# A softplus sum and its product in four chunks each, between the scans, in a state-space and expert kernel

## The reference, cut to what matters

```
xc = silu(conv(xi) + conv_b)
dt, Bm, Cm = split(xc @ W_x)
dt = softplus(dt @ W_dt + b_dt)
dA  = exp(dt[..., None] * A)
dBu = (dt * xc)[..., None] * Bm[:, :, None, :]
h   = scan over tokens of  h = dA * h + dBu
y   = einsum('blds,bls->bld', h, Cm) + D_skip * xc
```

## Time and profile before

| what | value |
|---|---|
| median of 3 runs | 1552.35 us (1552.22, 1552.35, 1558.31) |
| profiled execution, its own time | 1550.88 us |
| span of its trace | 1549.1 us |
| DVE busy | 1218.7 us (79%), 2149 instructions |
| PE busy (matmuls) | 1324.8 us (86%) |
| POOL busy | 1046.6 us (68%) |
| ACT busy | 786.5 us (51%) |

### The profile page before, as it was taken

The page is one execution under the profiler, slowest core; times in us unless marked ns, Lnnn a source line. Parts: engine busy times, 40 slices in busy tenths (PEclk is TensorE's granted clock), DMA queues, the critical chain, the costliest instruction groups (busy, mean ns, idle before and its releaser), DMA issues.

```text
span 1549.1 us, 26016 instructions
## 1 busy us (share of the span) xinstructions
PE 1324.8 (86%) x8010; PEld 1071.6 (69%) x8010; DVE 1218.7 (79%) x2149; ACT 786.5 (51%) x1385; POOL 1046.6 (68%) x943
## 2 busy tenths in 40 slices
PE   8567776877877998898798799979799999999997
PEld 3245465565565766657566666868799989999997
DVE  3798999999989899999999998988355545555554
ACT  3676767867866786786787687666000000000000
POOL 3585878899989789889999988987433452122222
PEclk9696998989969899999999999989999999999999
DMA  7212111323214344344343333677867797676672
GB/s 221 78 53 83 48 49 56 97 75 88 86 65 136 113 120 128 82 142 143 106 127 110 85 114 109 189 230 230 287 179 202 215 251 213 195 206 195 192 206 79
DMA packets 129345, 216.36 MB, mean 140 GB/s; under 512 B 17948, under 2 KB 74792, under 8 KB 129080
## 3 DMA queue, kind: packets, MB, share of 16 engines
q1 hardware_dynamic: 110376, 183.86, 38.6%
q0 software_dynamic: 16064, 27.62, 7.7%
q10 hardware_dynamic: 2768, 3.21, 0.8%
HBM read 178.34 MB, written 37.22 MB: 139 GB/s over the span
## 4 chain that ended last, share of the span: by engine, by line
PE 48%; DVE 16%; POOL 13%; ACT 10%; issue 9%; DMA 3%; SPq 1%; DVEq 0%; POOLq 0%; ACTq 0%
PE psum L1712 14%; PE psum L1728 13%; POOL dBu L883 9%; DVE w_sb L2013 8%; PE psum L1514 7%; ACT psum L1137 3%; DVE y L2024 3%; PE psum L1523 2%; PE psum L1480 2%; ACT hc L1121 2%; PE psum L1680 2%; PE psum L1667 2%; POOL rows_d L801 1%; POOL gT L732 1%; DVE w_sb L1994 1%
## 5 line engine op out<-in xcount | busy, mean ns | idle before, releaser
L883 POOL TENSOR_TENSOR dBu<-w_sb,brep 128x512 f32<-128x512 f32 x512 | 644.5, 1323 | 34.8 <-issue 16.0
L2013 DVE TENSOR_TENSOR_SCAN w_sb<-psum,dBu 128x512 f32<-128x512 f32 x512 | 611.2, 1211 | 57.5 <-ACT psum L1137 38.1
L1137 ACT ACTIVATE psum<-w_sb,aneg 128x512 f32<-128x512 f32 x512 | 350.4, 692 | 116.9 <-DVE w_sb L2013 114.4
L1514 PE MATMUL psum<-ident,w_sb 128*128 128x128 f32 x2048 | 303.3, 295 | 117.0 <-DVE y L2024 70.0
L1514 PEld LDWEIGHTS psum<-ident,w_sb 128*128 128x128 f32 x2048 | 248.3, 151 | 192.7 <-DVE y L2024 102.9
L870 POOL DMA_INDIRECT out<-dBu,token x59 | 92.3, 1564 | 303.6 <-DVE dBu L2229 152.5
L1121 ACT ACTIVATE hc<-psum,ct 128x512 f32<-128x512 f32 x256 | 175.1, 684 | 102.8 <-PE psum L1514 69.4
L1523 PE MATMUL psum<-ident,hc 128*128 128x128 f32 x1024 | 171.7, 299 | 33.5 <-ACT hc L1121 23.5
L1523 PEld LDWEIGHTS psum<-ident,hc 128*128 128x128 f32 x1024 | 133.0, 154 | 77.5 <-ACT hc L1121 36.5
L2024 DVE SCALAR_TENSOR_TENSOR y<-psum,ct,y 128x512 f32<-128x512 f32 x240 | 174.8, 728 | 12.9 <-PE psum L1514 12.3
L1712 PE MATMUL psum<-xgT,expert_pieces 128*128 128x128 f32 x960 | 113.9, 277 | 0.0
(11 more groups left out here) (274 smaller groups left out, 1757.7 us busy)
## 6 DMA issues: line engine op xcount, KB each, us to landing
brep<-b_d SPq DMA_DIRECT2D x128, 256.0 KB
expert_pieces<-in_W SPq DMA_DIRECT2D x30, 1024.0 KB
win<-in_W SPq DMA_DIRECT2D x29, 1024.0 KB
expert_pieces<-in_W SPq DMA_DIRECT2D x42, 512.0 KB, 5.9
dBu<-rows_d SPq DMA_DIRECT2D x35, 257.0 KB
w_sb<-in_W SPq DMA_DIRECT2D x8, 1024.0 KB
xg<-rows_d SPq DMA_DIRECT2D x22, 257.0 KB, 2.7
h_d<-hmod SPq DMA_DIRECT2D x8, 512.0 KB, 3.1
```

The costliest lines, as they stand in the source:

```text
L883: nc.gpsimd.tensor_tensor(dBu[:, i % RING, :], u[p][:, c, :], brep[:, s % 4, :], ALU.mult).then_inc(s_dBu, 1)
L1137: nc.scalar.activation(dA[:, i % DA_RING, :], dt[p][:, c, :], ACT.Exp, scale=aneg[:, c, s:s + 1]).then_inc(s_dA, 1)
L1514: last = nc.tensor.transpose(T[:, i // DT, c * P:(c + 1) * P], hs[s % 2][:, c, i * P:(i + 1) * P], ident[:, :])
L2013: nc.vector.tensor_tensor_scan(hs[s % 2][:, c, :], dA[:, i % DA_RING, :], dBu[:, (n * UNITS + i) % RING, :], 0.0, ALU.mult, ALU.add).then_ ...
```

## The change

The two operations are cut along the chunks. Pass 12 ends with the sums of chunks 0 and 1. In pass 13, the sum of chunk 2 follows scan 0, that of chunk 3 follows scan 1, the product of chunk 0 follows scan 2, and the product of chunk 1 ends the pass. In pass 14 the products of chunks 2 and 3 follow scans 0 and 1. The semaphores count chunks: ScalarE waits for all four sums as before, and GpSimd waits for the chunk that it needs next.

```diff
@@ gpsimd, inputs
-                    if s == 0 and has_before and c == 0:
-                        pool.wait_ge(s_u, n)
+                    if s == 0 and has_before:
+                        pool.wait_ge(s_u, (n - 1) * CH + c + 1)
@@ scalar, decays
-                        act.wait_ge(s_dt, n)
+                        act.wait_ge(s_dt, n * CH)
@@ vector
-            def dt_sum(n, p):
+            def dt_sum(n, p, c):
                 dve.wait_ge(s_sp, n)
-                nc.vector.tensor_tensor(dt[p][:, :, :], dt[p][:, :, :], u[p][:, :, :], ALU.add).then_inc(s_dt, 1)
-            def dt_x(n, p):
-                dve.wait_ge(s_dt, n)
-                nc.vector.tensor_tensor(u[p][:, :, :], dt[p][:, :, :], xc[p][:, :, :], ALU.mult).then_inc(s_u, 1)
+                nc.vector.tensor_tensor(dt[p][:, c, :], dt[p][:, c, :], u[p][:, c, :], ALU.add).then_inc(s_dt, 1)
+            def dt_x(n, p, c):
+                dve.wait_ge(s_dt, (n - 1) * CH + c + 1)
+                nc.vector.tensor_tensor(u[p][:, c, :], dt[p][:, c, :], xc[p][:, c, :], ALU.mult).then_inc(s_u, 1)
@@ vector, body
                     next_scan(s, 0)
+                    if has_p and s == 13:
+                        dt_sum(n + 1, 1 - p, 2)
+                    if has_p and s == 14:
+                        dt_x(n + 1, 1 - p, 2)
...
                     next_scan(s, 1)
+                    if has_p and s == 13:
+                        dt_sum(n + 1, 1 - p, 3)
+                    if has_p and s == 14:
+                        dt_x(n + 1, 1 - p, 3)
...
                     next_scan(s, 2)
+                    if has_p and s == 13:
+                        dt_x(n + 1, 1 - p, 0)
...
                     if has_p and s == 12:
-                        dt_sum(n + 1, 1 - p)
+                        dt_sum(n + 1, 1 - p, 0)
+                        dt_sum(n + 1, 1 - p, 1)
                     if has_p and s == 13:
-                        dt_x(n + 1, 1 - p)
+                        dt_x(n + 1, 1 - p, 1)
```

## The result

| | before | after |
|---|---|---|
| median of 6 runs each | 1552.28 us (1544.2 to 1558.31) | 1565.6 us (1561.86 to 1570.48) |
| ratio | | 1.008 [1.0048, 1.0111] |
| profiled execution, span | 1549.1 | 1567.7 (its own time 1569.51) |
| granted TensorE clock, mean of it | 0.930 | 0.921 |

The kernel after was run again later, with another set of runs of the kernel before: 1.009 [1.006, 1.0119]. Every ratio here leaves out single runs that stand over 1.5% above the fastest of their kernel, so it can differ in its last digit from the quotient of two medians.

A forecast was written before the change was run, and what follows sets the result against it. VectorE, full (15.60 of 16 us) around the sum and product, was taken as the bound. Carried costs of 12.4 us on 1550.88 gave 1563.3, 1564.8 on the runs' median footing, said as 1565; 8-of-10 range 1555 to 1573.

The forecast's parts named there:

- VectorE is the bound at the change: In the stretches holding the sum and product, VectorE is busy 15.60 of 16 us, so anything added there delays all that follows.
- Own time, +0.60 us per sequence: Eight 128x512 pieces at a 0.62 us pitch replace two whole operations at 2.18; +4.2 us in seven sequences.
- Waits for GpSimd: VectorE's pieces stand until about 0.12 us before a GpSimd operation in flight ends; 0.46 us per sequence was lost before.
- The walk: Piece-by-piece timeline of sequence 4 from the first sum, with waits for GpSimd's products; +1.6 or +2.1 us.
- the tie of the third sum: In sequence 4, third sum and GpSimd's product stream start together at about 2.45 us; if the product leads, it waits 1.05.
- Sequence 0, +1.8: First two sums wait 0.38 and 1.08 us for GpSimd, later pieces 0.10 in all; 15.25 against 13.47 us.
- The long second sum in sequences 0 and 3: Sign of being right: the second sum of the next sequence's chunks is among the long pieces, 1.2 to 1.75 us.
- What carries on: State 14's last scan ends +1.4 to +2.4 us later, so TensorE starts late; only sequence 3 has slack, 0.6 us.
- The sum, 12.4: Carried cost over seven sequences: 1.8 each in 0 to 2, 1.3 in 3, 1.9 each in 4 to 6.
- A: Rival: pieces' waits for GpSimd stay as small as now, only own time counts; +4.2 us, 1556 to 1558; chance 0.17.
- C: Rival: pieces meet two full and two half waits for GpSimd in each sequence; +23 us, 1575; chance 0.07.
- B: Rival: GpSimd's next-sequence products start about 1.8 us earlier and scans and gates gain; -8 us, 1544; chance 0.06.

## Why the prediction was right

1565 us was forecast, 1565.6 measured. Its steps:

- *VectorE is the bound at the change.* Right. Its timeline has no idle row between the first sum and the fourth product in any of the seven sequences, in either profile of the kernel after, and the scans wait for GpSimd 0.9 us once, before and after.
- *Own time, +0.60 us per sequence.* Mis-sized, one and a half times to twice too large. An undisturbed 128x512 lasted 0.66 us at a pitch of 0.583 (698.90 to 699.48), not 0.70 and 0.62. 8 x 0.583 - 2 x 2.18 = +0.30; the marks gave +0.41 with GpSimd's reading gone. I had taken the size of a 512 by subtracting from one 1024 seen in the preparation, and those 0.04 us, eight times, are the error against the pitches; the 0.1 us between them and the marks is not explained. That all of it is on the path does not hold for sequence 0, where idle time hid it. The Trainium skill's 58 cycles per operation ("VectorE: DVE Perf Modes", The TRN2 errata) give a pitch of 0.594 and, as an estimate, +0.36, nearer than my row.
- *Waits for GpSimd.* Right in mechanism and nearly in size. The walk had two outcomes at the tie of the third sum, and the second came: "the third sum waits 1.05", waits of 0.16, 0, 1.05, 0.50, 0, 0, 0.13, in sum 1.84 us; measured 0.13, 0.07, 1.01, 0.54, 0, 0, 0.18, 0, in sum 1.93. The distance from the first sum to the same scan is 706.12 - 690.76 = 15.36 us (15.0 or 15.55 in the walks). The rule behind it held at each of these, with a slightly smaller number: the wait ended 0.11 us before the end of GpSimd's product (0.06 to 0.07 beside its small steps), not 0.12 to 0.14, and a waiting GpSimd operation went in between two adjoining pieces. It does not hold everywhere. In sequence 0 of the kernel after with five idle statistics in sequence 4, whose code is the same up to there, the first sum began at 172.80 in the midst of a product and stood for three of them, 3.14 us, while GpSimd ran on at its undisturbed pitch of 1.23; the distance was 23.36 us for 20.93. Why it was passed over twice is open. VectorE's two sums, then GpSimd:

```profile
172.80 4.40 DVE L1999 TENSOR_TENSOR w_sb<-w_sb 128x512 f32<-128x512 f32 x2
```

```profile
169.85 6.19 POOL L883 TENSOR_TENSOR dBu<-w_sb,brep 128x512 f32<-128x512 f32 x5
```

- *Sequence 0, +1.8.* 0.41 and 1.10 for the first two sums (0.38 and 1.08 forecast); +1.66 us by the marks.
- *The long second sum in sequences 0 and 3.* Wrong for 3. It is in 0, 2, 5 and 6. In 2, 5 and 6 the half-clock stretch before has put VectorE elsewhere against GpSimd's stream; 3 behaves as 4 does.
- *What carries on.* Right in kind: TensorE's transposes waited 2.07 us for 0.19. The 0.6 us of slack in sequence 3 had no ground: it was read from a sequence behind a half-clock stretch, and in the kernel without GpSimd's reading sequences 3 and 4 take the same 20.4 us. The next distance lost another 0.3 us in sequences 4 and 5, which the sum did not have.
- *The sum, 12.4.* Locally it was some 13 to 14: 7 x 1.9, plus about 1 behind, or 1.3 less where sequence 2 costs 0.6 as in the second profile. It had too much own time and a little too little waiting in it. The medians give 13.3. The profiled pair's 18.6 holds two more half-clock stretches.
- *What I did not see:* that this stage has stretches in which TensorE's clock falls, worth 3 to 5 us each, a fourth or more of the whole effect. The profile before had one, at 528 us, and I passed over it. That the forecast came so near owes something to luck, since they come in both kernels in numbers that differ by execution. What is shown is the local cost; that the whole 13 us come from it is not.

*Rivals.* A (waits stay small) fell: the sums' middle duration is 0.906 us for 0.66 undisturbed, and the mean of all 56 pieces 0.90, over its 0.75. The middle of all 56, forecast near 0.75, is 0.67: the waits stand in few pieces, most of them sums. C (two full and two half waits) fell: one full and one half in sequence 4. B (GpSimd's route in the chain) fell in its own terms: GpSimd's first products of a sequence did start earlier (699.69, 8.9 us after the first sum, for 10.7), and no scan got anything from it. The 2.28 us of "issue" in the earlier trace rows was an idle engine that nobody waited for. The Trainium skill's rule on the read interface ("SBUF — State Buffer", Who interferes with whom) pointed at C, and gave the right mechanism; only the walk through the timeline gave the size.

## What to carry over

Cutting a two-input VectorE operation into pieces, beside a GpSimd stream that reads, can give GpSimd a door at a seam: before cutting, lay GpSimd's stream beside the pieces and count who stands, and avoid adjoining pieces of which the first releases GpSimd. On an engine that is full, a piece that lets a dependent start earlier is only worth something if the dependent is waited for; the waits of the bound engine show it, the chain of waits alone doesn't. Judge such edits by distances between marks in undisturbed sequences, since a total can move by half a per cent with TensorE's clock alone.

## What the runs showed of the hardware

- TensorE's granted clock fell to half for a part of states 11 and 12 in one to four of the sequences 1 to 7, in every kernel profiled here but the one that shares the product. The stretch then took 18.8 to 21.6 us for 15.0 to 15.9, and 1.0 to 1.7 us came back directly behind, in the two kernels compared. A fixed kernel shows it in nearly the same sequences each time (before 3, then 3, 4 and 7; after 2, 5 and 6, then 5 and 6), another kernel in others (sums alone in pieces: 4, 6 and 7). Sequence 0 stands apart: its states 11 and 12 took 16.1 to 16.3 us, with 9 to 13 us at half clock, in most profiles, and 14.1 to 14.2 us, with 3.4 us, in three. Kernels with the same code up to there are on both sides, so this differs by execution. The kernel before, then the kernel before with the idle statistics:

```profile
146.30:162.40 16.10, 14.98 (x58) 8.80 (x56) 13.60 (x23) 13.43 (x23) 8.34 (x8) 0.72 0.27 90
```

```profile
149.70:163.90 14.20, 11.49 (x55) 7.18 (x54) 13.38 (x24) 12.89 (x23) 6.37 (x7) 0.88 0.29 101
```

- I had written that no other VectorE operations of this stage exclude GpSimd's. That was wrong: a one-input operation of 128x4 in the kernel before took 1.68 us, all but its shortest 0.16 of it standing beside a GpSimd operation of 2.36 us. VectorE at that place, the eight of that line (ns), and GpSimd:

```profile
545.52 1.68 DVE L2078 TENSOR_SCALAR vd<-vd 128x4 f32<-128x4 f32 x1
```

```profile
L2078 DVE TENSOR_SCALAR vd<-vd x8: 161/404/1676, 283.5 to 1200.2; 128x4 f32<-128x4 f32 x8
```

```profile
544.80 2.36 POOL L763 TENSOR_TENSOR x<-x,y 128x1024 f32<-128x1024 f32 x1
```

The Trainium skill ("SBUF — State Buffer", Who interferes with whom) lists this form among those that can take the shared ports, and I had drawn only on its line on two inputs.
